# The last two groups of a state-space stage: gates and output projection in another order on TensorE

## The reference

```python
def reference(u, W_in, conv_w, conv_b, W_out, A_log, D_param, dt_bias, W_up, W_gate, W_down):
    x = u                                                    # (2, 2048, 512) float32
    x = x + 0.5 * ffn(layernorm(x), W_up, W_gate, W_down)    # ternary weights, silu(up) * gate
    x = x + mamba(layernorm(x), W_in, conv_w, conv_b, W_out, A_log, D_param, dt_bias)
    x = x + 0.5 * ffn(layernorm(x), W_up, W_gate, W_down)
    return x

def mamba(u, ...):                       # 8 heads of 64, state size 64, 4 taps
    z, x, B, C, dt = split(u @ W_in.T)
    x, B, C = split(silu(causal_conv(concat(x, B, C)) + conv_b))
    dt = softplus(dt + dt_bias); dA = exp(-exp(A_log) * dt)
    S = S * dA_t + dt_t * B_t x_t;  y_t = S C_t              # over 2048 steps, for each batch
    return ((y + D_param * x) * silu(z)) @ W_out.T
```

## Time and profile before

| | |
|---|---|
| median of 3 runs | 1781.74 us (1781.51 to 1782.21) |
| profiled execution | 1783.4 us, of which the span of its instructions 1781.6 us |
| busy share of the span | PE 98%, DVE 75%, ACT 53%, POOL 46% |
| mean granted clock of TensorE | 0.998 of full speed |
| state-space stage | from about 627 to 1178 us of the span |

### The profile page before, as it was taken

How to read it: one execution, slowest core, us unless ns; L and a number is a source line. 1 busy time by engine, 2 the same in 40 slices (tenths; PEclk the granted TensorE clock), 3 DMA queues, 4 the chain that set the end, 5 groups by cost and what they waited for, 6 DMA issues and landing times. The chain is left out here.

```text
span 1781.6 us, 35778 instructions
## 1 busy us (share of the span) xinstructions
PE 1748.4 (98%) x13280; PEld 1286.8 (72%) x13280; DVE 1339.1 (75%) x2317; ACT 942.9 (53%) x1421; POOL 821.9 (46%) x565
## 2 busy tenths in 40 slices
PE   6999999999999999999999999999999999999999
PEld 3588888888888844444444444655888888888888
DVE  7977777787775758778777777657887777877655
ACT  7744647456474465435435536334547465474653
POOL 2766426244262426456456456626244262452533
PEclk9999999999999999999999999999999999999999
DMA  7031130211303031111112112012121311112100
GB/s 330 24 90 43 47 88 16 72 41 47 88 23 120 0 104 33 57 42 62 56 35 68 56 36 69 30 65 42 48 43 47 88 41 47 41 47 65 41 24 24
DMA packets 125196, 104.49 MB, mean 59 GB/s; under 512 B 104000, under 2 KB 104512, under 8 KB 119744
## 3 DMA queue, kind: packets, MB, share of 16 engines
q1 hardware_dynamic: 125120, 103.60, 18.9%
HBM read 49.59 MB, written 25.17 MB: 42 GB/s over the span
## 5 line engine op out<-in xcount | busy, mean ns | idle before, releaser
L504 POOL TENSOR_TENSOR f_hlo<-f_h,f_hhi 128x768 f16<-128x768 f32 x135 | 201.3, 1491 | 602.9 <-ACT f_hhi L688 576.2
L1264 PE MATMUL f_gate_ps<-spare 128*128 128x256 f16 x2688 | 329.8, 272 | 0.4 <-DVE f_gate_ps L979 0.2
L1188 PE MATMUL f_down_ps<-wd,f_hhi 128*128 128x256 fp8e4 x1440 | 318.4, 273 | 2.6 <-POOL f_hlo L504 1.9
L1188 PE MATMUL f_down_ps<-wd,f_hlo 128*128 128x256 fp8e4 x1440 | 318.4, 273 | 0.0
L1264 PEld LDWEIGHTS f_gate_ps<-spare 128*128 128x128 fp8e4 x2688 | 254.7, 97 | 45.6 <-issue 2.1
L1264 PE MATMUL f_up_ps<-spare,wu 128*128 128x256 f16 x1792 | 229.9, 273 | 0.1
L1264 PEld LDWEIGHTS f_up_ps<-spare,wu 128*128 128x128 fp8e4 x1792 | 172.7, 98 | 23.3 <-issue 0.7
L883 DVE SCALAR_TENSOR_TENSOR xa<-f_down_ps,out_scale,xa 128x512 f32<-128x512 f32 x195 | 136.3, 743 | 62.3 <-PE f_down_ps L1188 62.0
L1650 POOL TENSOR_TENSOR s_am<-s_tri,s_al 128x512 f16<-128x512 f16 x128 | 155.3, 1243 | 21.4 <-DVE s_al L1922 18.8
L1188 PEld LDWEIGHTS f_down_ps<-wd,f_hhi 128*128 128x128 f16 x1440 | 140.9, 98 | 20.1 <-issue 3.7
L1188 PEld LDWEIGHTS f_down_ps<-wd,f_hlo 128*128 128x128 f16 x1440 | 140.9, 98 | 16.2
(11 more groups left out here) (247 smaller groups left out, 3293.7 us busy)
## 6 DMA issues: line engine op xcount, KB each, us to landing
xa<-res SPq DMA_DIRECT2D x16, 1024.0 KB, 5.3
res<-xa SPq DMA_DIRECT2D x15, 1024.0 KB, 3.9
res<-xa SPq DMA_DIRECT2D x34, 256.0 KB, 2.0
xa<-in_u SPq DMA_DIRECT2D x8, 1024.0 KB, 4.8
xa<-res SPq DMA_DIRECT2D x32, 256.0 KB, 2.7
late<-in_w_gate SPq DMA_DIRECT2D x4, 1024.0 KB, 17.2
spare<-in_w_up SPq DMA_DIRECT2D x3, 1024.0 KB, 9.0
late<-in_w_in SPq DMA_DIRECT2D x1, 2320.0 KB, 8.2
```

The lines of the kernel that those rows point to most:

```text
L504: last = nc.gpsimd.tensor_tensor(hlo[:, p, a:b, :], src, hhi[:, p, a:b, :], ALU.subtract)
L1188: last = nc.tensor.matmul(at, part[:, p, kind, m * P:(m + 1) * P], wd[:, weight, p, :], start=(p == 0 and part is hhi and (m == 0 or name ...
L1264: last = nc.tensor.matmul(acc[:, j * HT:(j + 1) * HT], w[:, k, e * P:(e + 1) * P], xop[part][:, o, k, :, :], start=(fresh and (j, k, part) ...
```

## The change

The last output projection of `EVE` is cut into three parts. Its first half (k = 0, 1) becomes the last thing of the group `EVE`, ahead of the wait for the masked decays; k = 2 stands where the whole projection stood, behind `chunk_start` of the first chunk of `LAST`; k = 3 stands behind `turn_x`, where the second half of that chunk's gates stood. Those gates are now computed whole in the last chunk of `EVE`, ahead of `sum_decays`. The waits of the projection stand ahead of its first part and its signal behind its last. Every other chunk and every other engine keeps its order.

```diff
--- before.py
+++ after.py
@@ -2185,14 +2185,16 @@
                                                         start=True, stop=True)
                             last.then_inc(st_done, 1)
 
-                        def project_out(g, c):
+                        def project_out(g, c, k0=0, k1=KD):
                             q = CH * order(g) + c
-                            pe.wait_ge(y4_done, after(q + 1))
-                            pe.wait_ge(res_done, after(q))
-                            for k in range(KD):
+                            if k0 == 0:
+                                pe.wait_ge(y4_done, after(q + 1))
+                                pe.wait_ge(res_done, after(q))
+                            for k in range(k0, k1):
                                 last = nc.tensor.matmul(out_ps[:, :], yv[:, k, :], wout[:, k, :],
                                                         start=(k == 0), stop=(k == KD - 1))
-                            last.then_inc(out_done, 1)
+                            if k1 == KD:
+                                last.then_inc(out_done, 1)
 
                         def group(g, front, ahead):
 
@@ -2206,7 +2208,7 @@
                                 if c:
                                     project_out(g, c - 1)
                                 elif g is LAST:
-                                    project_out(EVE, CH - 1)
+                                    project_out(EVE, CH - 1, KD // 2, KD - 1)
                                 if front is not None and c == 0:
                                     project_conv(front, 0)
                                 turn_x(g, c)
@@ -2217,8 +2219,10 @@
                                         sum_decays(front)
                                     if c:
                                         project_conv(front, c + 1, 0, KD // 2 if front is LAST else KD)
-                                if g is LAST:
+                                if g is LAST and c:
                                     project_z(g, c, KD // 2, KD)
+                                elif g is LAST:
+                                    project_out(EVE, CH - 1, KD - 1, KD)
                                 chunk_y(g, c)
                                 if front is not None and c == 0:
                                     project_dt(front)
@@ -2226,7 +2230,7 @@
                                 if front is LAST and c:
                                     project_conv(front, c + 1, KD // 2, KD)
                                     if c == CH - 1:
-                                        project_z(front, 0, 0, KD // 2)
+                                        project_z(front, 0)
                                         sum_decays(front)
                                 elif front is not None and c:
                                     project_z(front, c - 1)
@@ -2239,7 +2243,10 @@
                                 transposes(BEHIND, KD // 2, KD)
                             if front is not None and front is not LAST:
                                 project_z(front, CH - 1)
-                            if g is not EVE:
+                            if g is EVE:
+
+                                project_out(g, CH - 1, 0, KD // 2)
+                            else:
                                 project_out(g, CH - 1)
 
                         pe.wait_ge(late_in, 16 * N_LATE)
```

## The result

| | before | changed |
|---|---|---|
| median | 1781.72 us (20 runs) | 1784.78 us (20 runs) |
| profiled execution | 1783.4 us, span 1781.6 | 1784.79 us, span 1783.0 |
| idle time of TensorE, end of `EVE` to line 2171 | 3.62 us in one piece | 1.26 + 3.46 us |

The changed kernel is slower: ratio 1.0016, 95% interval 1.0010 to 1.0022, some 2.9 us, and within the 0.2% that were counted as no change. The median of 1784.78 us lies just over the top of the range (1784.6) and 1.6 us over the forecast. The two profiled executions are only 1.4 us apart; that the medians are 3.1 us apart is the thing to explain.

The account below looks back on a forecast made before the run. The prediction took TensorE's order of work as the time, with GpSimd's `s_cd` binding it at line 2171. It summed 1783.4 + 0.0 + 1.5 = 1784.9 us for the profiled execution, so 1783.2 as median, range 1781.2 to 1784.6.

Parts of the forecast that it names:

- What bounds it: Soon after the group border GpSimd's `s_cd` binds TensorE at line 2171, at 1135.87, by 0.14 us, before any change.
- (a): End of `EVE`: 3.60 us of moved work fills 3.62 us of idle time; sums for decays 1.88 us later, costing nothing.
- (b): Decays and chunk start after the border run at full clock, 1.74 us instead of 3.32: TensorE gains 1.58 us there.
- (c): First chunk of `LAST`: TensorE idles some 1.6 us before `turn_x`, then 2.4 to 3.4 us at line 2171 until `s_cd`.
- (d): GpSimd's chain to `s_cd` is unmoved, line 2171 stays at 1135.87 after new idle time: gain 0.0 us.
- the fourth case: VectorE's product on `s_lx` no longer holds GpSimd's masks: line 2171 up to 0.98 us earlier, 1780.8 to 1782.3; chance 0.06.
- (e): Around line 2171: a half-clock stretch follows the new idle time; +1.5 us taken, bounds 0 and 3.4.
- the sum's last one: From the profiled execution's 1784.9 us to the median: it stood 1.7 above the three runs' median 1781.74, so 1783.2.
- Rival 3: Slow clock holds on from line 2171 to 2133 of the next chunk: 1.7 us more, 3.4 in all, 1785.1; chance 0.08.
- Rival 1: GpSimd's `s_cd` binds line 2171 but no slow stretch falls behind it: 1781.7 us; chance 0.15.

Follow-up runs that it names:

- experiment 2: Changed kernel plus four unused matmuls (3.43 us) in the last group's first chunk, in TensorE's wait for `s_cd`: 1781.95 us, ratio 1.0002 to the kernel before.
- experiment 3: Kernel before plus the same four unused matmuls (3.43 us) in its 3.62 us of idle time ahead of line 2124: 1781.83 us, ratio 1.0002.
- experiment 7: Changed kernel with GpSimd's `s_cd` and `s_dtxe` ahead of the second chunk's masks in the first chunk of `LAST`: 1782.07 us, ratio 0.9999 to the kernel before.
- experiment 10: Kernel before plus 1.08 us of unused matmuls on TensorE at the end of the state-space stage: 1781.72 us, ratio 0.9998.
- experiment 1: The changed kernel timed again without any edit: 1785.73 us, median of 11 runs, ratio 1.0017 to the kernel before.
- the busy end: 1.08 us of unused matmuls added at the end of the state-space stage: 1783.31 us on the changed kernel, 1781.72 us on the kernel before.
- experiment 9: Changed kernel plus 1.08 us of unused matmuls on TensorE at the end of the state-space stage: 1783.31 us, ratio 1.0007 to the kernel before.
- experiment 6: Changed kernel with only the projection in three parts, the first chunk's second half of gates back ahead of `chunk_y`: 1783.48 us, ratio 1.0009 to the kernel before.
- experiment 8: Changed kernel with `s_cd`, `s_dtxe` ahead of masks, second chunk's gates behind first `chunk_y`, later gates one slot earlier: 1780.82 us, ratio 0.9987 to the kernel before.
- experiment 5: Changed kernel with only the first chunk's gates in the group ahead, the output projection whole in its old place: 1781.84 us, ratio 1.0004 to the kernel before.
- experiment 11: Kernel of experiment 8 plus 1.08 us of unused matmuls at the end of the state-space stage: 1779.40 us, ratio 0.9984 to the kernel before.
- experiment 4: Changed kernel with the second chunk's gates in the wait for `s_cd`, third and fourth chunks' gates one slot earlier: 1780.48 us, ratio 0.9992 to the kernel before.

## Why the prediction was right, and where it was off

**What bounds it** held: line 2171 waits for `s_cd`, whose end no work of TensorE moves (experiments 2 and 3), and comes 3.5 us sooner when GpSimd makes `s_cd` first (experiment 7). The profile of experiment 10, where the kernel before is unchanged up to there, names it: line 2171 stands at 1135.72 behind 0.21 us of idle time that `s_cd` ended.

**(a)** held. The 3.62 us went whole; the sums for the decays came 1.5 us later by the span's clock (1.88 was given) and held nobody.

**(b)** held: 1.76 us against 1.74.

**(c)** held in kind. The idle time ahead of line 2152 was 1.26 us instead of 1.6. Some 0.16 us of the difference are ScalarE's: the exponential for `s_lx` began 0.11 us behind the start of `s_dec`, and not 0.27. As much again is only the modelled end of the projection's part (1.02 us, where 0.86 was reckoned from start to start). The product on `s_lx` took 1.43 us and not the usual 1.23, with the rest of `s_dx` beside its start, and line 2164 came at 1131.15, ahead of the 1131.5 to 1132.4 given. Neither counts: what TensorE wins ahead of `s_cd` it waits.

**(d)** held: 3.46 us of idle time (the range ended at 3.4), line 2171 at 1135.70, which is 1135.87 less 0.16 by which the whole trace runs ahead. The masks took 5.01 us again though the product had moved, so the fourth case, a lighter hold by VectorE, fell. Experiment 7 moves the hold to `s_cd`: 2.03 instead of 1.27 us. The Trainium skill (SBUF — State Buffer, "SBUF: two separate sides") describes a lock that the first comer keeps for its whole instruction; both traces agree, with one instruction of GpSimd held for 0.98 and 0.76 us.

**(e)** held for the execution that it was reckoned against, +1.6 us behind line 2171 where +1.5 was taken, and 1784.79 us for 1784.9. This is luck in part: the profiled executions of both kernels happened to meet a slow stretch at the start of the next stage, and that of experiment 1, of the same kernel, came to 1786.12 us with a stretch twice as long.

**The step that failed is the sum's last one**, from the profiled execution to the median: "That execution stands 1.7 above the median of the three runs ... so 1783.2". I took the 1.7 us for a difference that would stay. They were the second slow stretch of the earlier trace rows, at the start of the feed-forward stage, which the profiled execution of the kernel before met and 52 of its 113 runs, by their times, did not. In the changed kernel nearly all runs meet it, again by their times: 28 of 30 stand at 1784.0 or above, and with the idle time there cut to 1.11 us nine of eleven stand at 1783.1 to 1783.5, which is the 1783.2 of the forecast. So for this kernel there was little or nothing to take off: 1784.9, the sum ahead of the last step, against the median of 1784.78. The term left out has this size: the busy end takes 0.45 us off the mean of the kernel before (1782.23 to 1781.78) and 1.56 us off that of the changed one (1785.04 to 1783.48), a difference of 1.1 us out of the 2.8 between the means. These means are of runs on different chips. Rows 6 had shown both stretches; I used the second only as evidence for what idle time does, and never asked whether the change would touch its odds. The chance of 0.13 that it gave to times outside the range is where the median fell.

**Rival 3** (the slow clock holds on) was given 0.08. One of the two profiles of the changed kernel shows it, 2.5 us lost in place of 1.6 (the rival had 3.4), and two of the eleven runs of experiment 9 have 1 us more than the others. Fourteen of 30 runs of the changed kernel stand over 1785: so 0.08 was too low, and what it should have been lies between 2 of 11 and 14 of 30. Rival 1 (no slow stretch behind `s_cd`) hardly occurs: two of 30 runs have a time that fits it.

Open stays why the changed kernel meets the stretch at the stage's start so much more often. Its runs show the two together and show that either can be taken away by itself; whether the one leads to the other none of them shows, and experiment 6 speaks against a plain rule: its profiled execution has both, but six of its eleven runs stand 1.6 us lower, with a time for one of the two only. Open too is why more runs of the changed kernel stand over 1785 us (14 of 30) than have a long stretch with the busy end (2 of 11).

## What to carry to other kernels

Before work is moved into an idle time, follow each other engine's chain to the next point where it binds the engine that is to be filled: the idle time moves to that point if the chain does not hang on the moved work. There it may cost more than where it was, because a stretch at half clock can be free ahead of a binding wait and is paid behind one: here 0 and 1.6 us for stretches of the same 3.4 us. What helped here was to give the binding engine another order (GpSimd's `s_cd` ahead of its masks) and to put other work into the wait that was then left (experiment 8). And ask of each slow stretch in a profile how many runs have it, before an execution's time is taken for the median.

## What the runs showed of the hardware

- 3.43 us of useless matmuls made the changed kernel 3.8 us faster (1785.73 to 1781.95 us on one chip): with work in the wait the profiled execution has no fall of the granted clock to 1.2 GHz behind it; without it, all three profiles of such kernels have one (3.4 us long in the first and in experiment 9, 6.7 in experiment 1).
- Idle time of 1.95 us was followed by a slow stretch 1.1 us after work had begun again (experiment 5), 2.01 us by one 0.5 us after (experiment 7), and three pieces of 1.72, 1.26 and 1.84 us by one (experiment 6). 1.62 us alone and 1.11 us alone had none behind them in the profiles (experiments 3, 9 to 11).
- Behind the same idle time of 2.19 us the stretch came in some runs and not in others: the profiled executions of experiments 2, 3 and 5 have full clock there, those of 4, 6, 7 and 8 a stretch of 3.4 us at half clock. By their times it came in 5 of the 11 runs of experiments 2 and 3 each.
